# A filling of unread TensorE products, in other tile shapes

## The reference

```
h = layernorm(x) * (1 + ca) + sa
x = x + ga * attn(h)        # layer norm, q/k/v, 16 heads of 16, causal band of 128, softmax, Wo,
                            # then layer norm, W1 (256 to 1024), gelu, W2, both with residual
h = layernorm(x) * (1 + cb) + sb
x = x + gb * ffn(h)         # sigmoid(xr @ Wr.T) * (relu(xk @ Wk.T)^2 @ Wv.T),
                            # xr, xk: mixtures of a row and the row before it
```

## Time and profile before

| what | value |
|---|---|
| runs of the kernel before | 685.73 and 689.19 us, median 687.46 |
| the profiled execution | given by its span, 683.1 us from first to last instruction; its own time is not among the two |
| PE busy | 588.2 us (86%), 6878 matmuls |
| DVE, ACT, POOL busy | 518.1, 508.8, 367.7 us |
| mean granted TensorE clock | 0.972 |

### The profile page before, as it was taken

The page is one execution under the profiler, slowest core; times in us unless marked ns, Lnnn a source line. Parts: engine busy times, 40 slices in busy tenths (PEclk is TensorE's granted clock), DMA queues, the critical chain, the costliest instruction groups (busy, mean ns, idle before and its releaser), DMA issues.

```text
span 683.1 us, 18212 instructions
## 1 busy us (share of the span) xinstructions
PE 588.2 (86%) x6878; PEld 470.8 (69%) x6878; DVE 518.1 (76%) x1075; ACT 508.8 (74%) x780; POOL 367.7 (54%) x514
## 2 busy tenths in 40 slices
PE   5785797998789898989989898989898988899986
PEld 2454586977576676768677767777676766777775
DVE  5566676777797799879987888798987688664553
ACT  2623655579798979897989798988898786894642
POOL 5203534481649564956576475837592657564231
PEclk9878999999999999999999999999999999999999
DMA  3734212232023132403231323222312222101010
GB/s 129 278 71 108 58 44 46 60 103 67 19 64 102 35 76 60 125 20 82 65 105 38 87 54 82 81 67 66 90 33 52 68 64 72 33 1 48 32 39 31
DMA packets 56867, 47.05 MB, mean 69 GB/s; under 512 B 26235, under 2 KB 48061, under 8 KB 56782
## 3 DMA queue, kind: packets, MB, share of 16 engines
q1 hardware_dynamic: 53798, 43.85, 24.1%
q10 hardware_dynamic: 2984, 2.05, 1.2%
HBM read 18.11 MB, written 4.23 MB: 33 GB/s over the span
## 4 chain that ended last, share of the span: by engine, by line
PE 45%; ACT 27%; DVE 9%; issue 8%; SPq 7%; DMA 2%; POOL 1%; ACTq 0%; DVEq 0%; POOLq 0%
ACT bank L946 6%; ACT p L878 5%; SPq L2186 4%; PE bank L429 4%; PE bank L467 4%; PE bank L455 3%; SPq L2188 3%; PE bank L430 3%; PE bank L431 3%; PE quad L327 3%; ACT hid_hi L956 3%; PE bank L232 3%; ACT L946 3%; PE quad L295 2%; ACT kt_hi L850 2%
## 5 line engine op out<-in xcount | busy, mean ns | idle before, releaser
L1950 POOL TENSOR_SCALAR_AFFINE_SELECT p<-p 128x448 f32<-128x448 f32 x64 | 40.1, 627 | 218.6 <-ACT p L878 179.0
L878 ACT ACTIVATE p<-quad,scale_s 128x768 f32<-128x768 f32 (+1 forms) x102 | 81.9, 821 | 38.4 <-PE quad L327 27.1
L893 ACT ACTIVATE p_hi<-p 128x1344 f16<-128x1344 f32 x64 | 83.9, 1322 | 14.3 <-POOL p L1955 7.1
L1963 POOL TENSOR_TENSOR p_lo<-p,p_hi 128x1344 f16<-128x1344 f32 x32 | 87.6, 2737 | 5.2 <-ACT p_hi L893 5.2
L1363 DVE TENSOR_REDUCE nmax<-quad 128x8 f32<-128x1032 f32 x64 | 78.9, 1233 | 2.2
L412 PE MATMUL bank<-bt_hi,w_hi 128*128 128x256 f16 x256 | 70.1, 274 | 10.5 <-DVE hid_lo L1436 9.0
L327 PE MATMUL quad<-q_st,k_st 100*128 100x192 f16 (+3 forms) x576 | 61.8, 231 | 19.6 <-ACT p L878 6.0
L1436 DVE SCALAR_TENSOR_TENSOR hid_lo<-bank,inv_f,hid_hi 128x512 f16<-128x512 f32 x64 | 47.9, 748 | 36.7 <-ACT hid_hi L956 36.3
L429 PE MATMUL bank<-w_hi,hid_hi 128*128 128x256 f16 x256 | 71.6, 280 | 1.3 <-DVE hid_lo L1436 1.2
L430 PE MATMUL bank<-w_lo,hid_hi 128*128 128x256 f16 x256 | 71.4, 279 | 0.0
L431 PE MATMUL bank<-w_hi,hid_lo 128*128 128x256 f16 x256 | 71.3, 279 | 0.0
(11 more groups left out here) (232 smaller groups left out, 1688.8 us busy)
## 6 DMA issues: line engine op xcount, KB each, us to landing
k_st<-kt_hi SPq DMA_DIRECT2D x120, 64.0 KB, 2.0
v_blk<-vn SPq DMA_DIRECT2D x64, 66.0 KB, 2.2
x<-x SPq DMA_DIRECT2D x16, 256.0 KB, 2.8
out<-x SPq DMA_DIRECT2D x16, 256.0 KB, 2.1
q_st<-qt_hi SPq DMA_DIRECT2D x120, 32.0 KB, 1.9
k_st<-kt_lo SPq DMA_DIRECT2D x60, 64.0 KB, 2.0
xa<-x SPq DMA_DIRECT2D x7, 512.0 KB, 4.3
stage<-w_ff SPq DMA_DIRECT2D x2, 1024.0 KB, 7.8
```

Source lines behind the costliest of these rows:

```text
L878: e.activation(p32[gp % 2][:, c0:c0 + 2 * w].rearrange("p (n c) -> p n c", n=2), quad[:, b0:b0 + 2, 0:w], ACT.Exp, scale=scale_s[:, 1:2]). ...
L893: e.activation(p_hi[gp % 2][:, :].rearrange("p (n c) -> p n c", c=GW)[:, :, 0:QW], p32[gp % 2][:, :].rearrange("p (n c) -> p n c", c=QW), ...
L1963: e.tensor_tensor(cut(p_lo), p32[gp % 2][:, :].rearrange("p (n c) -> p n c", c=QW), cut(p_hi), ALU.subtract).then_inc(s_plp, 1)
```

## The change

The call's product is kept at places with n%4 = 0 or 3, except place 3. At n%4 = 1 each product is replaced by two fp32 products of a column tile each: 128 rows, 64 columns of the identity as weights, 192 moving columns (64 columns read three times). At n%4 = 2 it is replaced by four with 32 columns of weights each and the same 192 moving columns. At place 3 it is replaced by four fp16 products in tiles of 64 rows by 64 columns, 192 moving columns each, from the value columns of wa_hi into banks 4 and 5; and the place waits until s_wvl is 2. The counts `times` stay as they are: 30 products fall under n%4 = 1, 41 under n%4 = 2, 3 under place 3, 87 stay. In the changed kernel the products are at lines 235, 239 (64 columns), 243 (32 columns) and 249 (place 3), and what lies behind is 18 lines further down.

```
--- before.py
+++ after.py
@@ -228,8 +228,26 @@
             def warm(n, times):
                 e.wait_ge(s_pool, POOL_IDENT)
                 e.wait_ge(s_peak, 3)
-                for _ in range(times):
-                    e.matmul(psum[5][:, 0:P], ident[:, :], ident[:, :], start=True, stop=True)
+                bank = psum[5]
+                wide = ident[:, 0:64].rearrange("p (o c) -> p o c", o=1).broadcast_to([P, 3, 64])
+                if n % 4 == 0 or n % 4 == 3 and n != 3:
+                    for _ in range(times):
+                        e.matmul(bank[:, 0:P], ident[:, :], ident[:, :], start=True, stop=True)
+                elif n % 4 == 1:
+                    for _ in range(times):
+                        for c in range(2):
+                            e.matmul(bank[64 * c:64 * c + 64, 0:192].rearrange("p (o c) -> p o c", o=3), ident[:, 64 * c:64 * c + 64], wide, start=True, stop=True)
+                elif n % 4 == 2:
+                    for _ in range(times):
+                        for c in range(4):
+                            e.matmul(bank[32 * c:32 * c + 32, 0:192].rearrange("p (o c) -> p o c", o=3), ident[:, 32 * c:32 * c + 32], wide, start=True, stop=True)
+                else:
+                    e.wait_ge(s_wvl, KC)
+                    for _ in range(times):
+                        for r, c in ((0, 0), (1, 1), (0, 1), (1, 0)):
+                            rows = slice(64 * r, 64 * r + 64)
+                            e.matmul(psum[(4, 5)[r]][64 * c:64 * c + 64, 0:192], wa_hi[rows, 0, 2 * D:2 * D + 64], wa_hi[rows, 0, 2 * D:2 * D + 192],
+                                     start=True, stop=True)
 
             def warm_end(n, times):
                 e.wait_ge(s_x1, NU)
```

## The result

The changed kernel takes 697.16 us (median of 2 runs, 696.38 and 697.94) against 687.46 before: ratio 1.0158, 95% interval 1.0121 to 1.0196. The forecast was 696. So it is slower, clear of the noise, and by less than 2%. The profiled run is the one of 696.38 us; its span is 694.6, so 1.8 us lie around the span. A second set of six runs beside the kernel before gave 698.89 against 686.24, ratio 1.0184 (1.0154 to 1.0213).

What follows compares the result with a forecast made beforehand. TensorE was taken as the bound, busy 588.2 of 683.1 us. Stretch by stretch, 1.5+0.9+3.0+3.2+1.6 = 10.2 us, less 1.5 for later waits, gave 8.7 on 687.5: 696 us, range 686 to 712.

Steps and rivals of the forecast that it cites:

- Side by side: Column tiles of a group overlap on TensorE, so a group of two or four costs 0.335 us.
- Changes of shape: Switching tile shape on TensorE costs about 0.1 us each, lower bound 0, upper 0.3; 28 are paid.
- Columns: 192 moving columns instead of 128 make each new group 0.112 us dearer than the product it replaces.
- Place 2: Ten filling products on the chain, mostly at half clock: 1.2 to 1.9 us more, taken as 1.5.
- Place 1: Three filling products before PE's 1.34 us wait for wa_lo: extension hidden.
- Place 3: Cheaper fp16 products, but PE waits for both value parts of wa_lo, delaying the third maxima: +0.9 us.
- 48 to 117 us: Longer filling and shape changes in this stretch, some hidden in waits: sum 3.0 us.
- 117 to 139 us: 20 products and 14 changes of shape, 3.9 us together, 0.65 covered by the wait at 138.94: +3.2 us.
- 139 to 158 us: Two changed places, of 7 and 5 products: 1.3 us and three changes of shape 0.3, together +1.6 us.
- After 160 us: Nothing is changed there; the delay is carried on, less 1.5 us for waits not caused by PE.
- The rival of the clock: Longer filling leaves less idle time, raising the granted clock; with slack after 160 us the time is 688; chance 0.18.

Runs made afterwards that it cites:

- e11: Changed kernel with each group of column tiles made one full-array fp32 product of 192 moving columns and place 3 as in the kernel before: 690.90 us, 1.0072.
- e4: Changed kernel with place 3 as in the kernel before, all other places as changed: 695.03 us, 1.0113.
- e3: Changed kernel with the two loops swapped at the 32-column places, so all products of one tile come before the next tile's: 716.77 us, 1.0436.
- e2: Changed kernel with every group of column tiles made one full-array fp32 product of the same 192 moving columns: 693.75 us, 1.0107.
- e5: Kernel before with only the n%4 = 2 places changed (groups of four 32-column tiles): 689.80 us, 1.0037.
- e6: Kernel before with only the n%4 = 1 places changed (groups of two 64-column tiles): 691.41 us, 1.0043.

## Why the prediction was right, and where it was not

It was right in its mechanism and nearly in its size, and part of the size is luck. In sum, at equal clock: forecast were 6.5 us of columns, 2.8 of changes of shape and 0.9 for place 3, 10.2 together, less 1.5 for waits later on, 8.7. Measured are 5.3 (e11), 4.0 (e4 less e11) and 1.0 ± 1.1 (both sets of the changed kernel less e4), 10.3 together. That 10.2 meets 10.3 is luck, columns too dear and changes of shape too cheap by 1.2 us each; the 1.5 taken off is what makes the forecast low. Term by term:

- *Side by side* held: 0.33 us a group of two or four, four first records within 0.1 us. The earlier trace rows had been the decisive ones: a wait for one tile that did not hold up the others. e3 adds the limit that the forecast had not asked for. The Trainium skill (TensorE: Matmul & The Clock Gate, Part 3, What overlaps and what doesn't) says that matmuls start strictly in program order. By an estimate from that rule, at the 0.16 us a record of this trace, the seven groups of place 30 would have taken 4.6 us. They took 2.41: the trace disagrees.
- *Changes of shape*: forecast 2.8 us for 28 paid ones at 0.1. The trace has 0.10 for one (the last score's 0.05 us of columns from 55.52 end at 55.57, the group starts at 55.67). In the total they are worth 4.0 ± 1.1 (e4 less e11) and 3.7 ± 1.2 (changed less e2): 0.14 each. Somewhat undersized.
- *Columns*: what is left of the forecast of 10.2 without the changes of shape (2.8) and place 3 (0.9) is 6.5; e11 measures 5.3 ± 0.6. Somewhat oversized. Place 2 is a small part of it: at full clock ten groups add 10 x 0.112 = 1.1 us instead of 1.5. In the profiled pair it added nothing: its ten groups took 3.39 us against the 3.88 of before, since the half-clock stretch that lay over it in the profile of before (from 33.5 to 36.9 us) was not there. In e11, where such a stretch lay over it too, it took 5.13, 1.25 more than before. Where the rest of the 1.2 us lies is not shown.
- *Place 1* was called hidden, behind 1.34 us of wait. In the changed kernel's profile nothing of that wait is left: its transposes took 1.94 us instead of 1.07, partly at half clock, and project(0) starts 0.42 us late (27.57). Place 2 took that back by its better clock, so the 0.00 at the second maxima is one clock against another and does not say that the change is free up to there.
- *Place 3*: the local step came out at 0.93 for 0.9. Its share in the total is 0.1 ± 0.6 alone and 2.4 to 4.9 us by the ratios beside the other changed places (e2 against e11, both sets of the changed kernel against e4), 2 of them by more time at half clock, of which the forecast knew nothing.
- *48 to 117 us*: +3.0 forecast; the table has 4.33-0.93 = 3.4 up to project(3). Two errors cancel in it: 0.9 given back at 69 us, and 1.1 by a half-clock stretch over values(1, 1) (2.30 us from first to last start instead of 1.19).
- *117 to 139 us*: +3.2 forecast, 3.76 measured. Here a step of the reasoning failed. I took 0.65 us of cover from the wait at 138.94, which the profile lays on the stacks' DMA. The changed kernel has the same wait, of the same 0.65 us, and names DVE:

```profile
144.66 0.35 PE L313 MATMUL quad<-kt_hi,qt_hi 32*32 32x320 f16 x16
...
145.65 1.23 DVE L1381 TENSOR_REDUCE nmax<-quad 128x8 f32<-128x1032 f32 x1
...
147.03 0.49 PE L345 MATMUL quad<-q_st,k_st 100*128 100x192 f16 x4 [0.65 <-DVE nmax L1381]
```

  In the kernel before, the same reduction ended at 138.79, 0.15 us ahead of the scores, as here (146.88 and 147.03):

```profile
137.56 1.23 DVE L1363 TENSOR_REDUCE nmax<-quad 128x8 f32<-128x1032 f32 x1
```

  The scores wait for two semaphores, the stacks and the bank. They happened to come within 0.1 us of each other. The bank's wait hangs on TensorE's own maxima 2.4 us earlier and moves with it: it covers nothing. And with TensorE 4 us later the copies on SP's queue left the chain altogether; from 121.57 to 147 it is TensorE's own work but for some 3 us, with 2.41 us of place 30 in it.
- *139 to 158 us*: 1.6 forecast, 9.46-8.09 = 1.37 measured.
- *After 160 us* I took 1.5 us off for waits that don't hang on TensorE. Next to nothing was given back: 9.45 us at 178 and 9.31 at 206, and at equal clock 9.8 and 10.5 for the whole kernel. Behind it the lag of the profiled pair goes up and down: to 10.8 at 251, behind a half-clock stretch that the changed kernel's run has at 247 us; to 12.4 at 329, where no half-clock stretch lies but the changed kernel waits for ACT and the kernel before doesn't; to 10.7 at 390, behind a half-clock stretch of before at 378; and by 0.7 more near 472, at another wait for ACT, to 11.5 at the end.

```profile
341.49 0.25 PE L345 MATMUL quad<-q_st,k_st 100*128 100x96 f16 x2 [1.02 <-ACT kc L870]
```

At the sum of 8.7 the forecast is 1 to 2 us low: the 0.65 and the 1.5 of cover were not there, and in the profiled pair the 1.5 of place 2 that didn't come hid most of this. The rival of the clock was half real: a longer filling does lower the time at half clock (e4, e5 and e11: 35 to 37 against 40, together 4.4 ± 2.8 less), worth 1 to 2 us, and with place 3 changed as well it is gone again. Longer 64-column places alone (e6, 41.6) don't lower it.

## What to carry to other kernels

Column tiles with 128 rows ran side by side in fp32 too, as long as neighbours in the program go to different tiles; price the group by one tile's columns and each change of shape with 0.10 to 0.14 us. Before a wait is counted as cover, look at every semaphore the instruction waits for: one that the engine itself releases over a neighbour moves with it and covers nothing. Filling that keeps the clock up has a best length; here two thirds of it was best of the four lengths. What its length costs and what its clock gives come apart only when runs are compared at equal time at half clock.

## What the runs showed of the hardware that was not expected

- The order of issue decides over the overlap of tiles: 3.39 us interleaved, 12.93 tile by tile (a quarter of it at half clock) for the same 80 records; with 2 records per tile no difference, with 14 (place 30) 7.36 against 2.41. TensorE started a record past three that waited for their tile, and not past more.
- A record of 32 columns of weights costs the same time as one of 128: 0.326 us median in e2's full-array records and in the tiles, and starts 0.16 us apart when they follow on one tile.
- The granted clock made no difference between column tiles and full arrays of the same length (36.7 and 37.0 us at half clock, the difference known to 6 us).
- The kernel before itself varies over 682.8 to 691.1 us, and its time at half clock explains three quarters of that scatter (a correlation of 0.86), at 0.28 us per us in its own runs and 0.31 over all kernels.
